# Weighted spreading: ScalarE casts the second part of an older unit ahead of the first part of the new one

## The chip, the core and the metric

One core of a Trainium2 chip runs the whole kernel. The time is the device time of one execution in microseconds; the number shown is the median of three runs.

## What is computed

Four graph layers over 12500 nodes with 48 features and 400000 edges, each as `x = x + layer(relu(layernorm(x)))`. All of them gather rows of a node table by one end of the edges, in places weight them, and add them up at the other end:

```python
xw = jnp.matmul(x, w)                                   # layer 0, edge_src = src
msgs = adj_vals[:, None] * xw[edge_src]
agg = jax.ops.segment_sum(msgs, edge_dst, num_segments=N_NODES)
...
for _ in range(NUM_LAYERS):                             # layer 2, two times
    x = spmm(edge_index, edge_weight, x, n)             # x[src] * edge_weight, summed by dst
    avg = avg + x * scale
...
def prop(h):                                            # layer 3, three times
    return jax.ops.segment_sum(w[:, None] * h[row], col, num_segments=n)
```

Layer 1 has a gate network on the edges beside it. Values are float32.

## The kernel before

Edges lie in blocks of 128 slots x 8 (a block has one window of 128 source nodes). Each gather of a layer is one call of `expand`, called a **spread** here: matmuls with one-hot matrices pick rows of the node table, the rows go to a staging buffer, and indirect stores put them in the order of the destinations into device memory. Each sum is a call of `collect`, which loads them in that order and adds them up with one-hot matmuls. Three spreads are **weighted**: layer 0 (width 80: 48 features and 32 extra columns, `extra`, stored as float32) and the two of layer 2 (width 48). They are followed by three **unweighted** spreads of layer 3, whose staging takes another branch of the same code.

Float32 values are carried by three bfloat16 parts whose sum is the value, since matmuls take bfloat16. A table has the three parts, so a pick is three matmuls added in PSUM. In a weighted spread the picked row is then multiplied by the edge weight, and the product has to be split in three parts again. A spread has 47 turns (`TURNS`) of 6 chunks (`RC`), a chunk is 2 blocks of 128 rows (`CH`) and 2 **units** (`UC`), 564 units in all. What happens to unit u:

- VectorE compares the chunk's loaded places with the partition number: one-hot matrices (`compare`, L1313, once a chunk). SyncE loads the places (L1226, a ring of 3 chunks where there are extra columns, else of 6).
- PE writes one identity matmul of 512 columns into the bank (L1263), then 24 one-hot matmuls (L1272), each 48 or 80 columns. There are `NW` banks: 2 in the first weighted spread, 3 in the others. Before them it waits until the bank's former unit is weighed (and, in the first spread, its extra columns copied).
- VectorE multiplies by the weight into `times`, another PSUM bank of four (`weigh`, L1322).
- ScalarE copies the extra columns (L1369, first spread only), and casts the product to bfloat16: the **first part** (`first_term`, L1372).
- PE subtracts the first part from the product in PSUM (**less-first**, `less_first`, L1244), in the program after the one-hot matmuls of unit u + 2.
- ScalarE casts what is left: the **second part** (`second_term`, L1377).
- VectorE subtracts that and casts: the **third part** (`third_term`, L1332).
- POOL issues an indirect store for each of the chunk's two blocks of 128 rows (L1412), one for each unit, when both units have their third part. Rows of padding are out of bounds and dropped.

The order on each engine is written out by hand in `turn`, with semaphores counting units: VectorE runs at step u the third part of unit u - 5 and then the weighing of unit u - 2; ScalarE handles at step u the first part of unit u and the second part of unit u - 2; PE the matmuls of unit u and less-first of unit u - 2. Each engine takes its instructions in this order.

Of the kernel before, what the change touches and what calls it, by code (L numbers as in the profile page):

```python
# [65 lines left out]
def gnn_kernel(nc, x, src, dst, edge_attr, edge_weight, node_type, node_vec, w0, b0, w1, b1, w2, b2,  # L66
# [56 lines left out]
    with ctx:  # L123
# [1048 lines left out]
        def expand(table, width, weighted, to_dram):  # L1172
# [20 lines left out]
            with ExitStack() as s:  # L1193
# [25 lines left out]
                with nc.Block() as block:  # L1219
# [144 lines left out]
                    def _(act):  # L1364
                        def first_term(i, first, c, n):
                            u = c * UC + n
                            act.wait_ge(x_times, i * UT + (bw + u + 1))
                            if extra:
                                act.copy(stage[:, c, n, ROW // 2:length].rearrange(  # L1369
                                            "p (a k f) -> p a k f", a=2, f=extra),  # L1370
                                         rows_of(u, D, width)).then_inc(x_extra, 1)
                            act.copy(terms(c, n, 0), left(u)).then_inc(x_first, 1)  # L1372

                        def second_term(i, c, n):
                            u = c * UC + n
                            act.wait_ge(x_rest, i * UT + (bw + u + 1))
                            act.copy(terms(c, n, 1), left(u)).then_inc(x_second, 1)  # L1377

                        def turn(i, first):
                            for c in range(RC):  # L1380
                                if not first:
                                    act.wait_ge(x_st[c], i * (16 * CH) + e * (TURNS * 16 * CH))
                                act.copy(row_d[:, c, :], idx_d[:, bass.ds(i * RG + c * CH, CH)]).then_inc(x_row, 1)
                                for n in range(UC):
                                    if weighted:
                                        first_term(i, first, c, n)
                                        u = c * UC + n
                                        if u >= 2:
                                            second_term(i, *before(u, 2))
                                        elif not first:  # L1390
                                            second_term(i - 1, *before(u, 2))
                                    elif n % 2 == 0:
                                        act.copy(*copy_out(act, i, first, c, n)).then_inc(x_out[0], 1)  # L1393
                        turns(act, TURNS, turn)
# [524 lines left out]
```

## Time and profile before

| | |
|---|---|
| median of 3 runs | 19425.97 us (19371.97 to 19426.68) |
| the profiled execution | 19498.8 us |
| its span, first to last instruction | 19497.0 us |
| busy: PE, VectorE, ScalarE, POOL | 12039.6, 12685.6, 5081.6, 7739.5 us |
| mean granted TensorE clock | 0.808 |
| weighted spreads | 7075 to 8342, 11229 to 12343, 12945 to 14064 us |

The profile is of one execution. A time in it is counted from the first instruction; PE is TensorE, DVE VectorE, ACT ScalarE, SP SyncE. A row of a group gives the line, the engine, the operation and its tiles, the number of instructions, their busy time and mean, and the engine's idle time just before them with what ended most of it. The names of the profile for the tiles: `exp_rows` is the picked rows in PSUM, `exp_times` the product, `exp_stage` the staging buffer, `h` the one-hot matrices.

### The profile page before, as it was taken

Reading aid. Unit: us, or ns where it says so; the run is one execution under the profiler, and the core shown is the slowest. Engines: PE = TensorE matmul, PEld = TensorE weight load, DVE = VectorE, ACT = ScalarE, POOL = GpSimd, SP = SyncE. Lnnn points to the kernel's source line nnn. Section 1 sums busy time; section 2 is a strip of 40 time slices with the busy share of each in tenths; the row PEclk is TensorE's granted clock in tenths of the full one; section 3 lists DMA queues with packets and bytes.
Section 4 is the critical chain, followed back from the end, with each engine's and each line's share of the span. In section 5 each row is a group of like instructions: output and inputs, shape, how many; then the busy total and the mean of one; then the engine's idle time right before and its main releaser. Section 6 shows DMA issues by size and latency. Waiting matters only on the chain. (4 is left out here: it accounts for less than half of the span.)

```text
span 19497.0 us, 597789 instructions
## 1 busy us (share of the span) xinstructions
PE 12039.6 (62%) x200859; PEld 9977.6 (51%) x203067; DVE 12685.6 (65%) x26741; ACT 5081.6 (26%) x14023; POOL 7739.5 (40%) x7745
## 2 busy tenths in 40 slices
PE   5666666666660056676776666666675676666667
PEld 4555555555550035564554545554564465455456
DVE  8555555555552246678997866776686676667666
ACT  0222222222222135502442044124303302311320
POOL 0555555555556624402331055125405613622640
PEclk7888888888875579998888988998895596588569
DMA  7444444444445648787998777777697888878877
GB/s 295 157 156 155 156 155 156 156 156 155 156 148 161 138 154 282 245 280 275 338 331 235 248 258 261 237 268 261 213 305 255 286 270 276 298 252 273 299 255 246
DMA packets 2039788, 4485.05 MB, mean 230 GB/s; under 512 B 383651, under 2 KB 820609, under 8 KB 2038903
## 3 DMA queue, kind: packets, MB, share of 16 engines
q1 hardware_dynamic: 1422358, 3108.06, 50.3%
q0 software_dynamic: 437168, 1034.15, 14.1%
q10 hardware_dynamic: 180144, 341.27, 4.8%
q8 instruction: 74, 1.21, 0.0%
q14 instruction: 44, 0.35, 0.0%
HBM read 2732.28 MB, written 2060.98 MB: 246 GB/s over the span
## 5 line engine op out<-in xcount | busy, mean ns | idle before, releaser
L1412 POOL DMA_INDIRECT messages<-exp_stage,exp_block_rows x2820 | 2992.9, 1061 | 5357.6 <-ACT exp_stage L1393 2403.5
L817 POOL DMA_INDIRECT records<-rec,row_i x3125 | 2992.0, 957 | 2868.1 <-DVE rec L683 2105.2
L1513 PE MATMUL sum_sums<-sum_slots,sum_onehot 128*128 128x48 bf16 (+1 forms) x94752 | 2728.4, 183 | 947.3 <-DVE h L1477 700.0
L1513 PEld LDWEIGHTS sum_sums<-sum_slots,sum_onehot 128*128 128x128 bf16 x94752 | 2569.5, 96 | 1227.8 <-issue 1226.3
L1278 PE MATMUL exp_rows<-tab,h 128*128 x13536 | 1843.8, 313 | 1214.3 <-issue 596.4
L1272 PE MATMUL exp_rows<-tab,h 128*128 x40608 | 1733.4, 194 | 1051.7 <-DVE exp_times L1322 430.3
L1278 PEld LDWEIGHTS exp_rows<-tab,h 128*128 128x128 bf16 x13536 | 1385.3, 136 | 1672.3 <-issue 1667.1
L737 PE MATMUL ps_l<-place,turned 98*128 98x98 f32 x6250 | 1131.3, 346 | 1745.2 <-ACT place L622 1741.2
L737 PEld LDWEIGHTS ps_l<-place,turned 98*128 98x128 f32 x6250 | 1019.1, 250 | 1832.7 <-issue 1832.7
L1272 PEld LDWEIGHTS exp_rows<-tab,h 128*128 128x128 bf16 x40608 | 1589.4, 100 | 500.6 <-issue 296.1
L683 DVE TENSOR_TENSOR rec<-ps_g,emeta 128x240 f32<-128x240 f32 x625 | 254.8, 408 | 2188.0 <-remote 1423.6
L1332 DVE TENSOR_TENSOR exp_stage<-exp_times,exp_stage 128x384 bf16<-128x384 f32 x1692 | 942.8, 557 | 1118.7 <-ACT exp_stage L1377 948.5
L1350 DVE CAST exp_stage<-exp_rows 128x576 bf16<-128x576 f32 x1410 | 1041.6, 754 | 909.0 <-PE exp_rows L1278 840.9
L1393 ACT CAST exp_stage<-exp_rows 128x576 bf16<-128x576 f32 x1692 | 1072.1, 639 | 1781.4 <-PE exp_rows L1278 1407.8
L1313 DVE TENSOR_SCALAR h<-exp_places,pcol 128x2048 bf16<-128x2048 bf16 x1692 | 1315.8, 778 | 31.9 <-DMA exp_places<-src_places 31.7
L624 ACT CAST turned<-ps_t 98x640 f32<-98x640 bf16 x625 | 432.5, 692 | 3306.9 <-remote 2852.6
L1765 POOL DMA_INDIRECT messages_back<-l_back,l_rows x564 | 556.3, 986 | 1590.2 <-ACT l_back L1642 842.7
L1372 ACT CAST exp_stage<-exp_times 128x384 bf16<-128x384 f32 x1692 | 812.9, 480 | 1225.6 <-DVE exp_times L1322 1029.2
L1483 DVE TENSOR_TENSOR sum_onehot<-sum_iota,drel 128x2048 bf16<-128x2048 bf16 x846 | 1035.6, 1224 | 61.4 <-issue 47.6
L1483 DVE TENSOR_TENSOR sum_onehot<-sum_iota,slots 128x2048 bf16<-128x2048 bf16 x846 | 1035.8, 1225 | 56.2 <-issue 44.7
L656 DVE SCALAR_TENSOR_TENSOR same<-win_row,emeta,lt_b 128x128 bf16<-128x128 bf16 x3125 | 1064.3, 341 | 1.6 <-DMA win_row<-src_windows_of_edges 1.6
L1477 DVE TENSOR_TENSOR h<-h,sum_sums 128x48 f32 x3384 | 683.0, 202 | 530.3 <-PE sum_sums L1513 275.7
(298 smaller groups left out, 21297.7 us busy)
## 6 DMA issues: line engine op xcount, KB each, us to landing
exp_places<-src_places SPq DMA_DIRECT2D x1692, 512.0 KB
sum_slots<-messages SPq DMA_DIRECT2D x1410, 576.0 KB, 5.2
messages_first<-fill SPq DMA_DIRECT2D x624, 375.5 KB
sum_slots<-messages_back SPq DMA_DIRECT2D x282, 600.0 KB, 5.2
messages_back<-fill ACTq DMA_DIRECT2D x624, 270.8 KB
sum_slots<-messages_first SPq DMA_DIRECT2D x282, 576.0 KB, 5.4
messages<-fill ACTq DMA_DIRECT2D x624, 260.0 KB
l_places<-dst_places SPq DMA_DIRECT2D x282, 512.0 KB
```

What stands on the lines that cost most here:

```text
L656: last = dve.scalar_tensor_tensor(out=same[:, g, j, j * P:(j + 1) * P], in0=win_row[:, g, j * P:(j + 1) * P], scalar=f[:, j, SWIN:SWIN + 1 ...
L737: last = pe.matmul(at(k), turned[0:W, bank[g], k * P:(k + 1) * P], place[0:W, :], start=False, stop=True, skip_group_check=True)
L817: pool.indirect_dma_start(rec_dram, bass.IndirectOffsetOnAxis(ap=row_i[:, g, k:k + 1], axis=0), rec[:, g, k, :], None).then_inc(put[g], 16)
L1272: last = pe.matmul(rows_at(u, a, k), of, flat[:, bass.ds(ws[g] * (3 * width) + j * width, width)], start=j == 0, stop=j == 2)
L1278: last = pe.matmul(got[:, u % NW, k // 2, at:at + 3 * D], of, flat[:, bass.ds(ws[g] * (3 * D), 3 * D)], start=True, stop=True)
L1313: dve.tensor_scalar(onehot[:, c % RS, :, :].rearrange("p n e -> p (n e)"), places[:, c % RP, :], pcol1[:, :], None, ALU.is_equal).then_inc ...
L1332: dve.tensor_tensor(terms(c, n, 2), left(u), terms(c, n, 1), ALU.subtract).then_inc(x_third, 1)
L1350: dve.tensor_copy(*copy_out(dve, i, first, c - 1, n)).then_inc(x_out[1], 1)
L1393: act.copy(*copy_out(act, i, first, c, n)).then_inc(x_out[0], 1)
L1412: pool.indirect_dma_start(to_dram, bass.IndirectOffsetOnAxis(ap=row_d[:, c, g:g + 1], axis=0), stage[:, c, g, :], None, bounds_check=last_ ...
L1483: dve.tensor_tensor(onehot[:, c % RS, :, :].rearrange("p n (e b) -> p n e b", b=2), iota[:, :].rearrange("p (e b) -> p e b", b=2).unsqueeze(1)
L1513: last = pe.matmul(sums[:, c % RS, g, 0:width], onehot[:, c % RS, g * B + k, :], of[:, n * width:(n + 1) * width], start=n == 0, stop=n == ...
```

## The change

Two statements of ScalarE's `turn` change places (the empty line stands in the changed file, and line numbers behind it grow by one).

```diff
--- before.py
+++ after.py
@@ -1383,12 +1383,13 @@
                                 act.copy(row_d[:, c, :], idx_d[:, bass.ds(i * RG + c * CH, CH)]).then_inc(x_row, 1)
                                 for n in range(UC):
                                     if weighted:
-                                        first_term(i, first, c, n)
+
                                         u = c * UC + n
                                         if u >= 2:
                                             second_term(i, *before(u, 2))
                                         elif not first:
                                             second_term(i - 1, *before(u, 2))
+                                        first_term(i, first, c, n)
                                     elif n % 2 == 0:
                                         act.copy(*copy_out(act, i, first, c, n)).then_inc(x_out[0], 1)
                         turns(act, TURNS, turn)
```

At step u ScalarE now first casts the second part of unit u - 2, then copies the extra columns and casts the first part of unit u. What stands in ScalarE's program in the first weighted spread, before (`exp_weighted` counts weighed units, `exp_less_first` less-first matmuls; a row with no wait follows the one above):

```order
L1383 COPY exp_block_rows<-idx_d 128x2
L1369 COPY exp_stage<-exp_rows 128x256 [waits exp_weighted]
L1372 CAST exp_stage<-exp_times 128x8x48
L1377 CAST exp_stage<-exp_times 128x8x48 [waits exp_less_first]
L1369 COPY exp_stage<-exp_rows 128x256 [waits exp_weighted]
L1372 CAST exp_stage<-exp_times 128x8x48
L1377 CAST exp_stage<-exp_times 128x8x48 [waits exp_less_first]
```

and with the change:

```order
L1383 COPY exp_block_rows<-idx_d 128x2
L1377 CAST exp_stage<-exp_times 128x8x48 [waits exp_less_first]
L1369 COPY exp_stage<-exp_rows 128x256 [waits exp_weighted]
L1372 CAST exp_stage<-exp_times 128x8x48
L1377 CAST exp_stage<-exp_times 128x8x48 [waits exp_less_first]
L1369 COPY exp_stage<-exp_rows 128x256 [waits exp_weighted]
L1372 CAST exp_stage<-exp_times 128x8x48
```

The cast L1377 with its wait for less-first stands before the copy L1369 with its wait for the weighing, and the row number copy L1383 stays at the head of each chunk. In the two later weighted spreads, before:

```order
L1383 COPY exp_block_rows<-idx_d 128x2
L1372 CAST exp_stage<-exp_times 128x8x48 [waits exp_weighted]
L1377 CAST exp_stage<-exp_times 128x8x48 [waits exp_less_first]
L1372 CAST exp_stage<-exp_times 128x8x48 [waits exp_weighted]
L1377 CAST exp_stage<-exp_times 128x8x48 [waits exp_less_first]
```

and with the change:

```order
L1383 COPY exp_block_rows<-idx_d 128x2
L1377 CAST exp_stage<-exp_times 128x8x48 [waits exp_less_first]
L1372 CAST exp_stage<-exp_times 128x8x48 [waits exp_weighted]
L1377 CAST exp_stage<-exp_times 128x8x48 [waits exp_less_first]
L1372 CAST exp_stage<-exp_times 128x8x48 [waits exp_weighted]
```

Here too L1377 moves ahead of L1372. VectorE's order in the same loop, which is the same in both kernels (`exp_second` counts second parts, `exp_rows` PE's units, `exp_load` the loads of places):

```order
L1313 TENSOR_SCALAR h<-exp_places,pcol 128x2048 [waits exp_rows,exp_load0]
L1332 TENSOR_TENSOR exp_stage<-exp_times,exp_stage 128x8x48 [waits exp_second]
L1322 TENSOR_TENSOR exp_times<-exp_rows,slots 128x384 [waits exp_third,exp_rows]
L1332 TENSOR_TENSOR exp_stage<-exp_times,exp_stage 128x8x48 [waits exp_second]
L1322 TENSOR_TENSOR exp_times<-exp_rows,slots 128x384 [waits exp_third,exp_rows]
```

The third part L1332 waits for ScalarE's second part, and the weighing L1322 of the next unit stands behind it.

## Rows read from the trace of the kernel before

**Rows 1.** The page, costliest groups: count, busy, mean ns, idle before.

```profile
L1332 DVE TENSOR_TENSOR exp_stage<-exp_times,exp_stage 128x384 bf16<-128x384 f32 x1692 | 942.8, 557 | 1118.7 <-ACT exp_stage L1377 948.5
```

**Rows 2.** The waits of the whole span: us in total, times, longest.

```profile
DVE exp_stage L1332 <- ACT exp_stage L1377: 948.5, 1134, 1.2
```

**Rows 3.** Timeline of the first spread: start us, us, engine, line.

```profile
7600.70 0.97 POOL L1412 DMA_INDIRECT messages_first<-exp_stage,exp_block_rows  x1 [0.30 <-issue]
...
7600.83 0.33 PE L1244 MATMUL exp_times<-exp_stage,less_ident_b 128*128 128x384 bf16 x1
...
7601.90 0.38 PE L1263 MATMUL exp_rows<-tab,ident_b 128*128 128x512 bf16 x1 [0.74 <-ACT exp_stage L1369]
...
7602.55 0.56 DVE L1332 TENSOR_TENSOR exp_stage<-exp_times,exp_stage 128x384 bf16<-128x384 f32 x1 [0.36 <-ACT exp_stage L1377]
7603.03 0.56 DVE L1322 TENSOR_TENSOR exp_times<-exp_rows,slots 128x384 f32<-128x384 f32 x1
...
7603.06 0.33 PE L1244 MATMUL exp_times<-exp_stage,less_ident_b 128*128 128x384 bf16 x1
7603.62 0.37 ACT L1369 COPY exp_stage<-exp_rows 128x256 f32<-128x256 f32 x1 [1.01 <-DVE exp_times L1322]
7603.89 0.48 ACT L1372 CAST exp_stage<-exp_times 128x384 bf16<-128x384 f32 x1
...
7604.10 0.10 PEld L1263 LDWEIGHTS exp_rows<-tab,ident_b 128*128 128x128 bf16 x1 [0.97 <-issue]
...
7604.26 0.50 ACT L1377 CAST exp_stage<-exp_times 128x384 bf16<-128x384 f32 x1
...
7604.78 0.56 DVE L1332 TENSOR_TENSOR exp_stage<-exp_times,exp_stage 128x384 bf16<-128x384 f32 x1 [1.20 <-ACT exp_stage L1377]
```

**Rows 4.** Timeline of the last weighted spread, columns as in rows 3.

```profile
13300.61 0.49 PE L1244 MATMUL exp_times<-exp_stage,less_ident_b 128*128 128x384 bf16 x1
...
13302.14 0.56 DVE L1332 TENSOR_TENSOR exp_stage<-exp_times,exp_stage 128x384 bf16<-128x384 f32 x1 [0.93 <-ACT exp_stage L1377]
...
13302.61 0.56 DVE L1322 TENSOR_TENSOR exp_times<-exp_rows,slots 128x384 f32<-128x384 f32 x1
...
13303.20 0.48 ACT L1372 CAST exp_stage<-exp_times 128x384 bf16<-128x384 f32 x1 [1.10 <-DVE exp_times L1322]
...
13303.25 0.49 PE L1244 MATMUL exp_times<-exp_stage,less_ident_b 128*128 128x384 bf16 x1
...
13303.58 0.48 ACT L1377 CAST exp_stage<-exp_times 128x384 bf16<-128x384 f32 x1
...
13304.09 0.56 DVE L1332 TENSOR_TENSOR exp_stage<-exp_times,exp_stage 128x384 bf16<-128x384 f32 x1 [0.27 <-issue]
...
13304.96 0.49 PE L1244 MATMUL exp_times<-exp_stage,less_ident_b 128*128 128x384 bf16 x1
```

**Rows 5.** Stretches: busy us (instructions) PE, PEld, DVE, ACT, POOL; clock, DMA, GB/s.

```profile
7200.00:8200.00 1000.00, 619.51 (x11373) 516.74 (x11596) 647.26 (x1115) 526.37 (x1563) 433.69 (x447) 1.00 0.79 278
13000.00:13900.00 900.00, 559.77 (x11568) 450.87 (x11796) 623.49 (x1133) 410.05 (x1133) 487.87 (x454) 0.89 0.78 261
14800.00:15600.00 800.00, 508.29 (x3704) 381.51 (x3704) 486.32 (x696) 313.71 (x695) 486.94 (x463) 0.55 0.85 291
9000.00:9500.00 500.00, 366.11 (x4886) 256.17 (x4884) 460.29 (x1033) 244.96 (x658) 184.33 (x188) 0.87 0.98 344
8400.00:8900.00 500.00, 386.32 (x12665) 343.82 (x12790) 417.53 (x787) 0.00 (x0) 0.00 (x0) 0.99 0.90 307
```

**Rows 6.** DMA share in slices of 25 us: 7300 to 8300, 13000 to 14000.

```profile
DMA  8778887787777877888777887887878887843333
...
DMA  7877777777877777777777777777788777787444
```

**Rows 7.** Lines L1412 and L1332: count, ns, first and last start us.

```profile
L1412 POOL DMA_INDIRECT messages_first<-exp_stage,exp_block_rows x564: 966/972/1300, 7083.9 to 8342.4; - x188
...
L1332 DVE TENSOR_TENSOR exp_stage<-exp_times,exp_stage x1692: 547/557/559, 7080.3 to 14063.5; 128x384 bf16<-128x384 f32 x188
```

## Prediction

> **What bounds the kernel now.** I read the page first, then the waits, then short timelines of the stretches that the change touches, then the busy time by stretch. On the page no engine fills the span, so the question is which wait ends last in the three weighted spreads. The costliest idle time in front of a VectorE instruction of these spreads stands before the third part (L1332): 1118.7 us over 1692 units [rows 1], of which the waits put 948.5 us down to ScalarE's cast of the second part (L1377) [rows 2]. The timeline of the first spread shows the ring that sets the pace [rows 3]. The third part starts at 7602.55, the weighing behind it at 7603.03, ScalarE's copy of the 32 extra columns at 7603.62, the first part at 7603.89, the second part at 7604.26, and the next third part at 7604.78: 0.48 + 0.59 + 0.27 + 0.37 + 0.52 = 2.23 us a unit. In the later two spreads the same ring without the extra copy takes 0.47 + 0.59 + 0.38 + 0.51 = 1.95 us [rows 4]. The stretches agree: 1000 us hold 447 units of the first spread (2.237 us each), 900 us hold 454 of a later one (1.982 us) [rows 5], one indirect store being one unit. A spread has 564 units [rows 7].
>
> The reader is to see one thing in rows 3: the second part that starts at 7604.26 had its input long before. PE leads by one unit, so the less-first matmul that this cast waits for is the one at 7600.83 (0.33 us), and ScalarE then stood idle for 1.01 us before 7603.62. The cast was ready, but stood in the program behind the first part of a newer unit, which waits for the weighing.
>
> **What the change takes away.** Nothing is added or removed: 1692 casts L1377 of 0.49 us change places with what stood before them (1692 casts L1372, and 564 copies L1369 in the first spread). No DMA, no semaphore and no buffer changes. The moved cast now runs in ScalarE's idle 1.01 us, beside the weighing. Two links leave the ring: VectorE's third part no longer follows extra copy, first part and second part, and with its input there it starts right behind the weighing. Cost of the cast in its new place: it holds ScalarE for 0.37 us from start to start; if it begins before the weighing ends it delays nothing. What is queued behind it is the extra copy, which frees PE's bank (the first spread has two). What remains is the ring over those two banks: 1.16 us from the identity load (7601.90) to the end of the unit's matmuls, where less-first starts (7603.06), a hand-off to VectorE, 0.59 us from the weighing to the extra copy, and about 0.5 us from that to the next identity load, 2.25 us and the hand-off. No row shows PE handing on to a VectorE that waits for it; the nearest are VectorE to ScalarE, 0.03 us after the end (7603.59 to 7603.62), and a whole matmul of 0.33 us with it, 0.36 us. I take the middle: 2.45 us for two units, 1.22 us each, and at either end under the bounds of the next part, so it costs nothing. If the extra copy is pushed back by the cast's full 0.37 us as well, the ring gives at most (2.61 + 0.37) / 2 = 1.5 us.
>
> **What is late next.** The gain ends where another limit takes over. Busy time per unit in the first spread: VectorE 647.26 / 447 = 1.45 us, PE 1.39, ScalarE 1.18; in a later one VectorE 623.49 / 454 = 1.37, PE 1.23, ScalarE 0.90 [rows 5]. POOL issues a store each 0.97 + 0.30 = 1.27 us [rows 3]. And the DMA: the share is 0.79 at 2.237 us a unit, so a unit costs 1.767 us of all 16 engines; in a later spread 0.78 x 1.982 = 1.546 us [rows 5]. These are larger than any engine's sum, so **the DMA becomes the bound**. How full can it be? The stage that sends messages back holds 0.98, the collect after the first spread 0.90 with nothing waiting on loads there that I could name; these are the nearest rows for the two ends [rows 5]. I take 0.97, near the first, because the loads of places are issued three chunks ahead in the first spread and six in the later ones, and the stores have six chunks of room, so that queues hold work all the time. That gives 1.767 / 0.97 = 1.82 us and 1.546 / 0.97 = 1.595 us a unit.
>
> The Trainium skill, "DMA: Bandwidth & Descriptors", section Specifications, gives about 358 GB/s as what the memory gives one core. The row at 0.98 moved 344 GB/s, a little under it [rows 5]. By that page's figure the estimate would be 278 x 2.237 / 358 = 1.74 us and 261 x 1.982 / 358 = 1.44 us a unit, and the gain some 920 us in place of the 735 below.
>
> At the end of each spread the DMA share falls to 0.3 to 0.4 (stores of padding rows are dropped): the last 6 slices of 25 us of the first spread and the last 3 of a later one [rows 6]. From 8150 to the last store at 8342.4 are 190 us or 86 units, from 13925 to the last third part at 14063.5 are 138 us or 70 units [rows 6, 7]. There the engine sums hold: 1.45 and 1.37 us.
>
> **The sum.** First spread: 478 units x (2.237 - 1.82) = 199, and 86 x (2.237 - 1.45) = 68: 267 us. Each later spread: 494 x (1.982 - 1.595) = 191, and 70 x (1.982 - 1.37) = 43: 234 us, twice 468. Together 735 us. The profiled execution took 19498.8 us, which gives 18764; it lies 73 us above the median of the runs shown, 19425.97, from which I subtract: **18691, rounded 18690 us**. The unweighted spreads and the collects are untouched: 0.
>
> The ends. With the DMA at 1.00 the units cost 1.767 and 1.546 us: gain 225 + 68 + 2 x (215 + 43) = 809. In the unweighted spreads, which move the same bytes, a unit costs 800 / 463 x 0.85 = 1.469 us of DMA against 1.546 [rows 5]; with packets that much (5%) quicker in both: 1.68 and 1.47 us, gain 334 + 2 x 296 = 926, time 18500. With 0.92 as a ceiling: 152 + 68 + 2 x (149 + 43) = 604, time 18820.
>
> **Rivals.**
> 1. *The spread settles at the pace of the unweighted one*, which has no such ring, the same bytes, and yet takes 1.728 us a unit at a share of 0.85 [rows 5]. For it: it is a measured pace with this traffic. Against: its clock is at 0.55, so PE is slower there than here. With a ceiling of 0.85: 2.08 us in the first spread and 1.728 in the later ones, gain 75 + 68 + 2 x (126 + 43) = 481, time 18945.
> 2. *The DMA does not bind*, the transfers fit under VectorE's 1.45 and 1.37 us: gain 564 x 0.787 + 2 x 564 x 0.612 = 1134, time 18290. Against it stands the share of 0.79, which would have to go to 1.22. The Trainium skill, same page and section, gives a fabric ceiling of 435 GB/s; by it a unit would need 1.43 and 1.19 us of DMA and this rival would hold. The highest row here, 344 GB/s at 0.98, speaks against it.
> 3. *The cast's wait only changes place.* ScalarE takes its instructions in order, and the moved cast waits for PE's less-first matmul; if PE loses its lead of one unit, this matmul comes only after the newest unit's matmuls, and the first part and extra copy stand behind it. The third part then gets its input as late as now: 0, time 19426. Against: idle 1.01 us before the extra copy, less-first done 3.1 us before the cast starts [rows 3]. The Trainium skill, "TensorE: Matmul & The Clock Gate", section on the array's architectural detail, says that ScalarE's queue is strictly first in, first out; that is the rule that speaks against putting a waiting cast in front.
> 4. *Slower: the clock.* The granted clock was 1.00 in the first spread, 0.89 in a later one, 0.55 in the unweighted ones [rows 5]. At the lower level (1.2 GHz) PE in a later spread needs 1.71 us between two less-first matmuls (13303.25 to 13304.96) and 4.35 us for two units with the window load between (13300.61 to 13304.96), 2.18 us each [rows 4]. Should the new rhythm hold the clock at the lower level through all three spreads: later ones + 0.2 x 1128 = + 224; the first, whose 24 matmuls have 80 columns for 48, about 2.18 + 24 x 32 / 1200 = 2.8 us at most, + 0.58 x 564 = + 330. Half of the sum of 554, some 275 us, gives 19700. It decides from a mean clock of about 0.6 downwards. Against it: PE's idle share shrinks with the change, it does not grow.
>
> **How the numbers follow.** DMA ceiling between 0.92 and 1.00, quicker packets included (18500 to 18820): 0.66. Rival 1: 0.15. Rival 2: 0.08. Something between 1 and 3: 0.03. Rival 3: 0.05. Rival 4: 0.03. The range, 18480 to 18960, takes in the forecast and rival 1. A measurement of this kernel can tell 0.3% (58 us) from no change. Faster by more: 0.66 + 0.15 + 0.08 + 0.03 = 0.92; same 0.05; slower 0.03.
>
> **What would show it.** In the changed profile the wait of L1332 for L1377 is gone or under 100 us; L1377 starts before L1372 of the newer unit and during the weighing; the DMA share of both spreads is 0.93 or more, at 1.8 and 1.6 us a unit; a new wait appears, VectorE's comparison (L1313) for the load of places, or ScalarE and SP for stores; the clock of the later spreads is above 0.89. I am wrong if the share stays near 0.8 (then an engine ring that I took for slack binds), or if L1332 still waits for ScalarE.

## The result and the profile after

| | before | changed |
|---|---|---|
| median | 19405.66 us (4 runs, 19371.97 to 19426.68) | 19631.73 us (4 runs, 19629.64 to 19639.83) |
| ratio, 95% interval | 1 | 1.0123 (1.0106 to 1.0139) |
| span of the profiled execution | 19497.0 us | 19627.9 us |
| mean granted clock | 0.808 | 0.795 |

The forecast was 18690 us, in a range of 18480 to 18960. The change is slower, by 226 us, where a gain of 735 us was predicted. The wait that I set out to remove is gone, but the spreads got longer. The waits of the whole span with the change (us in total, times, longest) answer to [rows 2]; line numbers behind L1391 have grown by one:

```profile
ACT exp_stage L1377 <- PE exp_times L1244: 1399.4, 549, 5.8
...
DVE exp_times L1322 <- PE exp_rows L1272: 1156.8, 502, 5.5
...
DVE exp_stage L1332 <- ACT exp_stage L1377: 19.3, 36, 1.2
```

The third part's wait for the second part fell from 948.5 us [rows 2] to 19.3. In its place ScalarE waits 1399.4 us for PE's less-first matmul and VectorE's weighing 1156.8 us for PE's one-hot matmuls. In the kernel before the first of these two does not occur and the second is small (waits of the whole span, kernel before):

```profile
DVE exp_times L1322 <- PE exp_rows L1272: 11.7, 16, 1.1
```

On the page of the changed kernel, in the columns of [rows 1]:

```profile
L1272 PE MATMUL exp_rows<-tab,h 128*128 x40608 | 1974.3, 202 | 535.6 <-issue 522.5
```

The stretches, columns as in [rows 5]:

```profile
7200.00:8200.00 1000.00, 726.81 (x10868) 560.60 (x10868) 568.76 (x1044) 498.84 (x1462) 412.99 (x418) 0.85 0.74 260
13100.00:14000.00 900.00, 617.33 (x10969) 443.36 (x10970) 573.50 (x1055) 399.82 (x1055) 417.39 (x421) 0.87 0.72 242
```

The first spread does 418 units in 1000 us (2.39 us each, 2.237 before), a later one 421 in 900 (2.14 us, 1.982 before). The DMA share fell, from 0.79 to 0.74 and from 0.78 to 0.72; I had wanted 0.93 or more. The clock fell in the first spread from 1.00 to 0.85.

What happens inside is seen in the timeline. First a good stretch of the first spread (start us, us, engine, line, in brackets the idle time before it):

```profile
7602.27 0.55 DVE L1332 TENSOR_TENSOR exp_stage<-exp_times,exp_stage 128x384 bf16<-128x384 f32 x1
...
7602.47 0.49 ACT L1377 CAST exp_stage<-exp_times 128x384 bf16<-128x384 f32 x1
...
7602.74 0.56 DVE L1322 TENSOR_TENSOR exp_times<-exp_rows,slots 128x384 f32<-128x384 f32 x1
7603.20 0.55 DVE L1332 TENSOR_TENSOR exp_stage<-exp_times,exp_stage 128x384 bf16<-128x384 f32 x1
```

Here everything is as the prediction has it: second part L1377 beside the weighing, third part L1332 right behind it, two third parts 0.93 us apart. Now the stretch 12 us earlier, in which two units pass through PE:

```profile
7589.38 1.11 PE L1272 MATMUL exp_rows<-tab,h 128*128 x24
...
7590.33 0.33 PE L1244 MATMUL exp_times<-exp_stage,less_ident_b 128*128 128x384 bf16 x1
...
7590.50 0.38 PE L1263 MATMUL exp_rows<-tab,ident_b 128*128 128x512 bf16 x1
7590.71 0.70 PE L1272 MATMUL exp_rows<-tab,h 128*128 x15
...
7591.61 0.23 PE L1272 MATMUL exp_rows<-tab,h 128*128 x2 [0.20 <-issue]
7592.36 0.28 PE L1272 MATMUL exp_rows<-tab,h 128*128 x3 [0.52 <-issue]
...
7593.09 0.30 PE L1272 MATMUL exp_rows<-tab,h 128*128 x4 [0.46 <-issue]
7593.23 0.33 PE L1244 MATMUL exp_times<-exp_stage,less_ident_b 128*128 128x384 bf16 x1
7594.64 0.48 ACT L1377 CAST exp_stage<-exp_times 128x384 bf16<-128x384 f32 x1 [4.22 <-PE exp_times L1244]
7594.83 0.57 DVE L1322 TENSOR_TENSOR exp_times<-exp_rows,slots 128x384 f32<-128x384 f32 x1 [4.07 <-PE exp_rows L1272]
...
7595.95 0.38 PE L1263 MATMUL exp_rows<-tab,ident_b 128*128 128x512 bf16 x1 [2.39 <-ACT exp_stage L1369]
```

The weighing at 7594.83 belongs to the first of the two units, whose 24 matmuls stand in one piece and end in the record at 7590.49; the cast at 7594.64 belongs to the less-first matmul that ends at 7590.66. Both consumers stood for 4 us after work that the record calls done. Meanwhile the second unit's 24 matmuls come in pieces, 15, 2, 3 and 4, with gaps in which PE waits for nothing that the profile names ("issue"); its weighing comes at 7595.77. The trace also holds the semaphore events, that is, the moments at which PE's **signal** "this unit's matmuls are done" is raised. The first unit's signal comes at 7594.58, 4.1 us after the recorded end, and the second's at 7594.85, 0.27 us behind it. The kernel before has the same in its later two spreads: of their signals 369 in 886 come less than 0.5 us after the one ahead, where the recorded last matmuls of two units are never less than 0.98 us apart. So the signals come late and in pairs, which is not the recorded pace of the matmuls; what holds them up, no row shows. The unit pace comes from long and short intervals between weighings: in the first spread a tenth are under 0.94 us, half under 1.66, and a tenth over 5.15, where before nearly all were 2.23.

Grouped by me: a unit's last matmul start to the start of its weighing, over 444 middle units of each spread, and the gaps over 0.15 us between the matmuls of one unit, summed over the whole spread (to some 2%):

| spread | unit us | last matmul to weighing, median / 90% | gaps, us |
|---|---|---|---|
| before, first | 2.242 | 2.23 / 2.23 | 0 |
| before, later two | 1.983, 1.987 | 2.02 / 2.22, 2.00 / 2.18 | 127, 138 |
| changed, first | 2.390 | 1.35 / 3.71 | 155 |
| changed, later two | 2.143, 2.137 | 1.87 / 3.88, 1.71 / 3.93 | 279, 301 |

The third column is a wait only where VectorE stood idle. In the changed first spread that is so for 213 of the 444 units (median 1.40, 90% under 4.37 us), in the later two for 190 and 180 (median 3.46 and 3.58 us).

Before, the ring of casts kept VectorE from asking for PE's result until about 2.2 us after its last matmul started. Lateness up to that left no wait. It did leave late signals: in the kernel before, the signal of each chunk's first unit comes 1.33 us (median) after the recorded end in the first spread and 1.5 us in the later two, that of the second unit 0.01 to 0.03 us after it. With the change a tenth of the signals come more than 3.3 to 3.6 us late.

### The profile page after: what moved, and what is told of

Its sections match the earlier page's. It is cut to its first block and busy times, and to the rows that moved or that the text cites. A ratio compares the mean times of both kernels' runs of the same rounds, so it can differ in the third digit from the quotient of the medians.

```text
span 19627.9 us, 599996 instructions
## 1 busy us (share of the span) xinstructions
PE 12795.6 (65%) x203066; PEld 10186.7 (52%) x203067; DVE 12658.7 (64%) x26741; ACT 5140.9 (26%) x14023; POOL 7663.3 (39%) x7745
## 5 line engine op out<-in xcount | busy, mean ns | idle before, releaser
L1413 POOL DMA_INDIRECT messages<-exp_stage,exp_block_rows x2820 | 2906.4, 1031 | 5563.0 <-ACT exp_stage L1394 2440.3
L1278 PE MATMUL exp_rows<-tab,h 128*128 x13536 | 1802.8, 311 | 1202.1 <-issue 484.2
L1272 PE MATMUL exp_rows<-tab,h 128*128 x40608 | 1974.3, 202 | 535.6 <-issue 522.5
L1272 PEld LDWEIGHTS exp_rows<-tab,h 128*128 128x128 bf16 x40608 | 1764.6, 106 | 990.5 <-issue 808.2
L1278 PEld LDWEIGHTS exp_rows<-tab,h 128*128 128x128 bf16 x13536 | 1384.9, 136 | 1619.7 <-issue 1613.0
L1322 DVE TENSOR_TENSOR exp_times<-exp_rows,slots 128x384 f32<-128x384 f32 x1692 | 951.9, 563 | 1413.1 <-PE exp_rows L1272 1156.8
L1313 DVE TENSOR_SCALAR h<-exp_places,pcol 128x2048 bf16<-128x2048 bf16 x1692 | 1367.5, 808 | 32.2 <-DMA exp_places<-src_places 31.4
L1377 ACT CAST exp_stage<-exp_times 128x384 bf16<-128x384 f32 x1692 | 817.1, 483 | 1631.1 <-PE exp_times L1244 1399.4
L1263 PE MATMUL exp_rows<-tab,ident_b 128*128 128x512 bf16 x1692 | 762.3, 451 | 511.6 <-issue 223.7
```

The source lines that it names most:

```text
L1272: last = pe.matmul(rows_at(u, a, k), of, flat[:, bass.ds(ws[g] * (3 * width) + j * width, width)], start=j == 0, stop=j == 2)
L1278: last = pe.matmul(got[:, u % NW, k // 2, at:at + 3 * D], of, flat[:, bass.ds(ws[g] * (3 * D), 3 * D)], start=True, stop=True)
L1313: dve.tensor_scalar(onehot[:, c % RS, :, :].rearrange("p n e -> p (n e)"), places[:, c % RP, :], pcol1[:, :], None, ALU.is_equal).then_inc ...
L1322: dve.tensor_tensor(left(u), rows_of(u, 0, D), ews[:, bass.ds(i * (2 * RG) + 2 * (c * CH + n), 2), :].unsqueeze(3) .to_broadcast([P, 2, BH ...
L1413: pool.indirect_dma_start(to_dram, bass.IndirectOffsetOnAxis(ap=row_d[:, c, g:g + 1], axis=0), stage[:, c, g, :], None, bounds_check=last_ ...
```

## The experiments

After the result three explanations were open: transfers in the way (of PE's instructions, or of its window loads), something in PE's own stream, and the clock. A kernel is named by its label. Where it says "with the change", the kernel is the changed one with that edit. "The kernel before on that chip" is the one timed beside it.

**The first set (e1 to e4, with the change)** makes the transfers of a weighted spread small, takes the window numbers out, or takes matmuls away.

```diff
# e1_small_loads (and e9), SyncE; fewer places than needed are loaded
+ few = CH * P * B if first or not weighted else P
- sp.dma_start(places[:, c % RP, :], ...)
+ sp.dma_start(places[:, c % RP, 0:few], ...)
# e2_small_stores (and e10), POOL; most rows are out of bounds and dropped
- last_block = pool.to_reg(NBLK - 1)
+ last_block = pool.to_reg(P - 1 if weighted else NBLK - 1)
# e3_fixed_windows (and e12, e18), PE; the same windows for every block
- ws = windows(PE_ENGINE, win_s, i * RG + c * CH, CH)
+ ws = (c, c + 7) if weighted else windows(PE_ENGINE, win_s, ...)
# e4_third_of_matmuls (and e11), PE; one of three parts is picked
- for j in range(3):
+ for j in range(1):
```

> The changed kernel, but from the second turn of each weighted spread on the load of places moves 128 of the 2048 columns (one-hot matrices are built from old places, so the messages are not the reference's). In the changed kernel PE stands still for 155, 279 and 300 us inside its groups of 24 matmuls in the three weighted spreads, against 0, 127 and 138 us before, and a spread takes 2.39, 2.14 and 2.13 us a unit. Theory A, the transfers hold PE up (the loads by what they take of memory and of the ways to it): stalls under 30 us a spread, units at 1.5 us in the first and 1.4 us in the others, total about 18500 us. Theory B, PE's instruction stream cannot be supplied faster than this, whatever the DMA does: stalls stay at 250 us or more, units at 2.1 us or more, total 19500 to 19650 us. Theory C, the window load at the head of each chunk sets the pace: the stalls inside groups may go, but a unit stays at 2.0 us or more.

> The changed kernel, but in the weighted spreads the bound of the indirect stores is 128 blocks rows, so nearly all rows are dropped (the sums of these layers are then not the reference's); POOL issues as before. Theory A in the form that the loads alone do it: stalls stay near 155, 279 and 300 us. Theory A in the form that any transfer does it: stalls fall by half or more and a unit to 1.6 to 1.8 us, total about 18900 us. Theory B: no change, total 19500 to 19650 us.

> The changed kernel, but in the weighted spreads PE takes constant windows of the table instead of loading their numbers (other rows are picked, so values are not the reference's): no register load of about 0.54 us and no address arithmetic on PE. Theory C, the window load sets the pace: a unit falls to about 1.6 us, total about 18800 us. Theory B: the stream is shorter by some 10 of 120 instructions a chunk: a unit falls by 0.1 to 0.2 us, stalls stay. Theory A: a unit falls by the 0.3 us a unit that the load leaves open, to 2.1 and 1.85 us, and the stalls inside the groups stay or grow.

> The changed kernel, but a picked row is one bfloat16 part instead of three in the weighted spreads: 8 one-hot matmuls a unit instead of 24 (values lose accuracy). All transfers are as before. Theory B, the supply of PE's instructions: a unit has 22 instructions instead of 54, the stalls go and the unit falls to what the DMA or VectorE allows, 1.6 to 1.85 us, total about 18750 us. Theory A, the transfers hold PE up wherever it is: stalls per spread stay above 100 us, a unit falls by the PE time left out (0.4 to 0.6 us) at most.

Measured: 16379.86, 16330.06, 16450.09 and 16346.72 us. But the kernel before took 17388.26 us there, not 19400: this chip was in another condition, in which every variant looks alike, and the four totals tell nothing about the slower result. I had not foreseen that, and my reading against the 19400 level would have been wrong. What they do show is PE handing on promptly: in e1's first spread the last matmul to the weighing takes 0.36 us at the median and 0.46 at 99%, gaps sum to 2 us, and the units take 1.64 us (1.35 in the later spreads). e3, with all its transfers in place, runs at 1.67 and 1.37 us.

**The second set (e5 to e7)** repeats both kernels, and puts the new order into the first spread alone.

```diff
# e7_first_spread_only, ScalarE's turn
+ if not extra: first_term(i, first, c, n)
  u = c * UC + n
  ... second_term ...
+ if extra: first_term(i, first, c, n)
```

> The changed kernel once more, beside the kernel before. The last four runs were made where the kernel before takes 17388 us, not 19406; so what they show has to be set against the changed kernel in the same place. Theory A, what takes the transfers' time also holds PE up, and that differs from place to place: where the kernel before takes about 17400 us the change is faster, by my sum for DMA at 0.97 to 1.00 about 650 to 800 us, with stalls inside PE's groups under 30 us a spread; where it takes about 19400 the change is slower again by some 200 us. Theory B, PE's instruction supply is the bound whatever the transfers do: slower by about 1% in either place, stalls of 150 us and more in each spread.

> The kernel before, for a profile in the same place as the changed kernel's. Both theories: units of 2.23 us in the first spread and 1.95 to 1.98 us in the others, since the ring through ScalarE's second part sets them. Theory A: where the whole takes about 17400 us no stalls inside PE's groups in any spread (0, 127 and 138 us before); Theory B: 100 us and more in the later two wherever it runs.

> The new order in the first weighted spread only. Theory A in a place of about 17400 us: a gain of 250 to 350 us, the later spreads as before; in a place of about 19400 us: a loss of 60 to 90 us. Theory B: a loss of 60 to 90 us in either.

The changed kernel took 19651.53 us against 19354.99, ratio 1.0146 (1.0129 to 1.0163). e6, which is the kernel before, took 19352.42. e7 took 19425.65, ratio 1.0045 (1.0029 to 1.0061). The ledger closes with e6 and the changed kernel's first profile: the three weighted spreads take 1256, 1108 and 1108 us from first to last store in e6, and 1344, 1202 and 1199 with the change, together 273 us more, of 277.3 us in the spans. In e7 only the first spread is slow (2.364 us a unit, 1.972 in the later ones as before), 71 us in all. So the new order costs time in the first spread by itself and does not slow the others from there; that each of the later two loses some 90 us is the difference between e6 and the changed kernel.

**The third set (e8 to e11, with the change)** repeats three of the edits on a chip where the kernel before takes 19499.34 us.

> The changed kernel beside the shortened ones of this group. Theory A: slower by 1.0 to 1.5% where the kernel before takes about 19400 us, with 150 to 300 us of stalls inside PE's groups a spread; faster by 3 to 5% where it takes about 17400 us, with under 10 us of stalls. Theory B: slower by about 1% in both.

> The changed kernel with loads of places of 128 columns from the second turn on (old places are used, values are not the reference's), in the same place as e8. Where the kernel before takes about 19400 us, Theory A (transfers and PE disturb each other): stalls fall from 155, 279 and 300 us to under 30 us a spread and a unit to 1.65 and 1.35 us, as in e1. Theory B (PE's supply of instructions is slow there by itself): stalls stay above 150 us and a unit above 2.0 us. Where it takes about 17400 us: as e1.

> The changed kernel with nearly all rows of the weighted spreads' stores dropped, in the same place as e8. Where the kernel before takes about 19400 us, Theory A with any transfer: stalls fall by half or more; Theory A with loads alone: they stay; Theory B: stay, unit above 2.0 us. Where it takes about 17400 us: as e2.

> The changed kernel with 8 one-hot matmuls a unit instead of 24 (one of three parts; values lose accuracy), in the same place as e8. Where the kernel before takes about 19400 us, Theory B: the stalls go, and a unit falls to 1.4 to 1.85 us. Theory A: PE has fewer matmuls but is held up wherever it is, a unit falls by the PE time left out, 0.4 to 0.6 us, to 1.6 to 1.9 us, stalls above 50 us. Where it takes about 17400 us: as e4.

The changed kernel took 19896.51 us (ratio 1.0195, 1.014 to 1.025), with small loads 19971.9, with small stores 19903.69, with a third of the matmuls 19246.39. Stretches of e9, e10 and e11:

```profile
7200.00:8200.00 1000.00, 660.63 (x10306) 548.39 (x10510) 550.29 (x1012) 483.31 (x1417) 399.01 (x405) 0.84 0.40 156
```
```profile
7200.00:8200.00 1000.00, 665.18 (x10439) 551.50 (x10641) 555.65 (x1022) 487.37 (x1431) 404.08 (x409) 0.85 0.34 107
```
```profile
7200.00:8200.00 1000.00, 576.23 (x4838) 368.43 (x4920) 664.83 (x1229) 590.17 (x1720) 489.08 (x491) 0.69 0.83 286
```

With the DMA share down to 0.40 and 0.34, the units still take 2.47 and 2.44 us, as they did with all transfers (2.469 in e8), and the gaps in PE's groups sum to 146 and 130 us against 152. That rules the transfers out as the bound, and loads and stores each by itself as what holds PE up; both small at once was not run. The same hold-up stands in e10's timeline: VectorE stands idle for 4.07 us before a weighing at 7604.67, for matmuls recorded as done at 7600.40 whose signal comes at 7604.44.

With 8 matmuls a unit for 24 (e11) the gaps are gone (0 us), the first spread does 491 units in 1000 us, and the kernel is 3.3% shorter than e8 and 1.3% shorter than the kernel before on that chip, at a clock of only 0.69. So **PE's stream binds the changed spreads**, and a lower clock does not undo the gain; fewer instructions, fewer columns and a shorter loop come together in this edit, so it does not say which of them counts. Nor does it take the hold-up away. A unit takes 2.04 us in the first spread (outside what either theory gave, 1.4 to 1.85 and 1.6 to 1.9) and 1.82 in the later ones, where the same program takes 1.62 and 1.36 at the 17400 level (e4), and VectorE still waits for PE, for 571.1 us in the whole span where e4 has 26.6:

```profile
DVE exp_times L1322 <- PE exp_rows L1272: 571.1, 318, 4.3
```

**The fourth set (e12 to e15, with the change)** was to tell apart what in PE's stream does it: window numbers in registers, POOL's stores, or the identity matmul. In e13 the windows are loaded and then replaced by fixed ones; in e14 POOL's loop is `range(RC if not weighted else 0)` and the waits for these stores go; no message of the weighted spreads is stored then; in e15 the identity matmul at L1263 goes, and the one-hot matmuls start their sums by themselves (`start=j == 0`).

> The changed kernel with constant windows on PE in the weighted spreads (other rows are picked, values are not the reference's): no load of window numbers and no addresses from registers. So far, where the kernel before takes about 19400 us: the changed one takes 2.39 to 2.47, 2.13 to 2.2 us a unit whether loads or stores are cut down or not (e9, e10), and matmul results come up to 4.5 us after the last matmul's recorded start, against 0.36 us in e1. Theory B1, PE gets matmuls with register addresses late there: units fall to 1.9 us or less in the first spread and 1.6 or less in the others, no stalls inside groups. Theory B2, PE gets any instruction late there: units fall by 0.1 to 0.3 us, stalls stay. If it runs where the kernel before takes about 17400 us: 1.67 and 1.37 us as in e3.

> As e12, but PE still loads the window numbers, and then uses constants. Tells the register load from the register addresses. Theory B1 in the form of the addresses: as e12. Theory C, the load with what it makes wait (0.54 to 1.4 us once a chunk): as the changed kernel, 2.1 to 2.4 us a unit.

> The changed kernel without indirect stores in the weighted spreads (their messages are left out): POOL does nothing there. Theory D, POOL's work of issuing holds up the others (it was there in e10, where only the rows were dropped): units fall below 1.7 and 1.5 us. Theories B: no change, 2.1 to 2.4 us.

> The changed kernel without the identity matmul of 512 columns ahead of a weighted unit's matmuls. Theory E, PE is bound by its columns, at a lower real rate than recorded: 512 of 2816 and of 2048 columns are gone, units fall by 0.4 to 0.5 us where the kernel before takes about 19400 us. Theories B: 2 of 54 instructions a unit are gone, a unit falls by 0.1 us at most, stalls stay. The granted clock may fall below 0.85, since PE does less.

Measured: 16437.39, 16377.73, 16220.45 and 16506.69 us. The chip, which had taken 19354.99 us for the kernel before in the second set, now took 17433.89, so the condition is not a property of the chip. At this level the fourth set does not tell its suspects apart either. It shows the DMA share that I had predicted; e12:

```profile
5800.00:6300.00 500.00, 394.83 (x7796) 320.19 (x7793) 396.77 (x750) 353.89 (x1049) 323.50 (x300) 1.00 0.99 378
9600.00:10000.00 400.00, 337.00 (x7578) 254.70 (x7573) 382.73 (x729) 273.03 (x730) 306.77 (x294) 1.00 0.99 378
```

The DMA share is 0.99, at 300 units in 500 us and 294 in 400. But other limits lie close behind: e1, whose small loads bring the share down to 0.60 and 0.53, takes 1.64 and 1.35 us a unit for 1.67 and 1.37. Without stores (e14) it is 1.505 and 1.316 us, near VectorE's 1.45 and 1.37 of my sum, with VectorE busy for 0.92 and 0.97 of the time. e15, which leaves out nothing that the result needs, is 5.3% shorter than the kernel before beside it; it is a single run, at the 19400 level it was not tried, and its units (1.74 and 1.45 us) are longer than e12's, so nothing here shows that leaving the identity matmul out helps.

**The fifth set (e16 to e18)** repeats both kernels and puts fixed windows to the test at the 19400 level.

> The changed kernel, with the kernel before timed beside it. Where the kernel before takes about 17400 us: faster by 5 to 6%, about 16450 us, units of 1.67 and 1.37 us with the DMA at 0.99, no stalls (e12 and e13, which differ from it by constant addresses alone, took 16437 and 16378 us there). Where it takes about 19400 us: slower by 1 to 2%.

> The kernel before, for a profile in the same conditions as e16. Where it takes about 17400 us: weighted units still 2.23 and 1.95 us (the ring sets them, not PE), no stalls inside PE's groups, and the time less than 19400 comes from the first stage and the unweighted spreads. Where it takes about 19400: as e6.

> The changed kernel with constant windows on PE in the weighted spreads (values are not the reference's). Where the kernel before takes about 19400 us, which is where it has not run yet: Theory B1, PE gets matmuls with register addresses late there: 1.9 and 1.6 us a unit or less; Theory B2, PE's stream of matmuls is slow there whatever the addresses: 2.1 us or more, stalls stay. Where it takes about 17400 us: 1.67 and 1.37 us as before.

The changed kernel took 19650.37 us against 19368.47, ratio 1.0139 (1.0112 to 1.0165), e17 19416.57, and e18 19563.64. A stretch of the first spread of e18 (e17's holds 447 units at a clock of 1.00, as before):

```profile
7200.00:8200.00 1000.00, 723.69 (x11437) 552.11 (x11435) 600.28 (x1099) 527.22 (x1539) 434.60 (x440) 0.87 0.76 265
```

Fixed windows take 0.10 and 0.05 us off a unit (2.282 and some 2.09, against 2.384 and 2.14 in e16), and the gaps stay (127, 347, 333 us). They are not the cause (B1, register addresses in the matmuls, and C, the window load, are out). But e12 and e18 are one kernel on two chips, and that comparison says most:

| e12 and e18, one kernel | e12 | e18 |
|---|---|---|
| total | 16437.39 us | 19563.64 us |
| unit, first and later weighted spreads | 1.67, 1.37 us | 2.28, 2.09 us |
| gaps inside PE's groups, three spreads | 2, 0, 1 us | 127, 347, 333 us |
| first stage (3125 stores of records) | 4012 us | 5298 us |
| unweighted spreads | 764, 762, 760 us | 948, 957, 955 us |
| the first four collects | 528, 550, 548, 549 us | 528, 549, 549, 549 us |
| messages sent back | 1497 us | 1501 us |

The collects and the sending back, which are full of transfers, do not differ by 0.5%. The first stage and all spreads differ by 24 to 53%. The clock was lower in e18's spreads (0.87, 0.81, 0.79 for 1.00), but of the intervals over 3.5 us between two weighings in the changed kernel's first spread only about a quarter touch a stretch at the lower of the clock's two levels, 1.2 GHz, where the spread spends 29% of its time; in the later two 53 and 43% touch one, with 31 and 25% of the time there. Most long intervals of the first spread lie wholly at full clock, as does the one in the timeline above, so there the clock is not what makes them; in the later two, where long intervals touch the lower level more often than its share of the time, it may add to them.

**What stays open** is why PE's stream is held up, and its results late, in one condition and not in the other. Two more readings narrow it. The page of the changed kernel has few packets that bring instructions, 74 on one queue and 43 on another:

```profile
q8 instruction: 74, 1.21, 0.0%
```

Those of both queues start at 6998 to 7047 us for the first spread and then none before 8370, so no fetch by DMA falls into the loop. And the long intervals prefer places in the program: a turn has 12 units, and in the last weighted spread of the changed kernel the mean interval before a chunk's first unit is 4.22, 2.25, 3.85, 2.19, 3.72 and 2.22 us over the six chunks, alternating, with 1.04 to 1.45 us for the second units. Over some 37 turns that does not come from chance, but a rhythm of two chunks, once begun, would also keep its places, so it need not be the program's places that cause it. How PE is supplied with instructions is one suspect. Against the plain form of it, that PE cannot get them fast enough, stands the first collect: it runs 13536 matmuls in 528 us at both levels, 26 in each us, where the changed kernel's first spread has 11. e11 shortens the loop body and takes matmuls away in one step, and the two were not tried apart. What delays PE's signals is another suspect. Each run comes with a span and a clock, so all were recorded as they ran, and whether recording PE's many small instructions takes part in it was not tried. POOL's issuing (e14) and the identity matmul (e15) ran only at the 17400 level, so they are untested as causes too. The changed kernel without any edit was never seen at that level; that it gains there is argued from e13, whose windows are loaded as before and which took 16377.73 us against 17433.89, and not shown.

## Why the prediction was wrong

- **What bounds the kernel before**: right. The ring third part, weighing, copy, first part, second part held in e6 and e17 to a hundredth (2.236 and 1.973 us a unit, for 2.237 and 1.982).
- **What the change takes away**: right. The cast runs beside the weighing, the wait of the third part is gone (948.5 to 19.3 us), and the moved cast delays next to nothing: with the change ScalarE takes up a newly weighed unit 0.03 us (median) after the weighing ends.
- **The ring that remains**: here the prediction failed. "No row shows PE handing on to a VectorE that waits for it" was true of the rows, and I then bounded the hand-off from PE to VectorE by 0.03 and 0.36 us and wrote that the ring costs nothing. Measured with the change, the time from the last matmul's start to the weighing is 1.35 us at the median and 3.71 at 90% in the first spread. By my own formula, (1.16 + x + 0.59 + 0.5) / 2 us a unit: with 0.36 it gives 1.3, with 1.35 it gives 1.8, with 3.71 it gives 3.0, and the measured mean is 2.39. The mean of x is 1.60 and gives 1.9, so the hand-off is the larger part but not all; gaps inside the groups (155 us over 564 units, 0.27 each) and the clock of 0.85 lengthen the 1.16 as well, and how much of the rest is theirs was not taken apart. That e1 shows 0.36 us too at the 17400 level is luck: I had built it from a less-first matmul and another hand-off. The cause of the failure is that I priced a resource from places where somebody waits for it, and almost no one waited for PE: in the first spread VectorE asked 2.2 us after the last matmul began. The trace of before did have the price. In the 15 places inside a spread where VectorE stood idle for PE, the last matmul had started 2.7 to 3.6 us earlier, and PE's signals were late in every second unit.
- **PE's sum**, 1.39 and 1.23 us a unit: wrong as a bound, because it adds recorded durations. Neither the gaps between pieces of a group nor the time from a recorded end to the moment the result can be used stands in it. A trace of it was in the profile of before and I did not read it: 127 and 138 us of gaps in the later two spreads, which the lead of one unit hid.
- **The DMA becomes the bound**: wrong at this level (0.74 and 0.72, for 0.97). At the other the share is 0.99 as I had it (e12), but with 0.60 and 0.53 (e1) a unit is only 0.03 and 0.02 us shorter, so VectorE and the ring were as near a bound. There a unit costs less of the DMA than my 1.767 and 1.546 us: 1.67 x 0.99 = 1.65 and 1.37 x 0.99 = 1.36 us, since the packets of the loads take 183 ns in the first spread for 217 before. The prediction's end with quicker packets had 1.68 and 1.47. A small misreading goes with it: the share of the first spread falls in the last five slices of [rows 6], from 8175 us on, and not in six; that is worth 4 us of the 735.
- **Rival 1** (the pace of the unweighted spread, 2.08 us) came nearest in kind: it took that pace as a limit that no sum explains. In the table of e12 and e18 that spread differs between the levels too, 948 us for 764. I gave it 0.15, and excused it by its clock.
- **Rival 2** (the DMA does not bind) and **rival 3** (the wait changes place): the wait did move to L1377 for less-first, as rival 3 has it, but because PE is late, not because ScalarE's order blocks: over all three spreads of the changed kernel a weighed unit stood behind an idle L1377 for some 4 us in all. The price of 0 was too low by 226 us. The Trainium skill's rule that ScalarE's queue is first in, first out ("TensorE: Matmul & The Clock Gate", architectural detail) is in agreement with the order seen, and cost nothing by itself: in e3 and e12, with fixed windows at the 17400 level, the same order gains.
- **Rival 4** (slower by the clock, 0.03): right in sign, but its mechanism needed a mean clock of about 0.6, and the spreads had 0.83 to 0.87. What I set against it, that PE's idle share shrinks, came true (PE's recorded busy share went from 0.62 to 0.73 in the first spread, in part because it ran slower), and the clock fell from 1.00 to 0.85 all the same. So that argument did not hold, and why the clock fell is not shown.
- **The memory's limit.** At the 17400 level the stretches moved 378 GB/s at a share of 0.99. The Trainium skill ("DMA: Bandwidth & Descriptors", Specifications) gives some 358 as the memory's limit for one core, half of what two cores share; this kernel's one core went above it, so the measurement decides against it as a limit here. The fabric ceiling of 435 from the same section was not reached.
- Not foreseen at all: that taking a wait away would make the spread slower than the ring it had. The steady ring of 2.23 us gave PE a lead of one unit that absorbed its hold-ups. With the new order VectorE consumes early when it can, the lead is used up, and each hold-up of 3 to 4 us then stands in full, while the few banks hold too few units for the short intervals to make up for it.

The last sentence is the explanation that I hold. Shown of it are that VectorE now stands idle for PE, the late signals and the dependence on PE's matmuls (e11). That the banks keep the short intervals from making up is argued: the later spreads have three banks for two and lose as much (94 and 91 us for 88). And it leaves one thing open: the hold-ups themselves grew. In the first spread of before no signal in the 444 middle units came more than 2.9 us late, with the change a tenth are over 3.3 us, so the new order does something to PE's stream beyond laying its delays bare.

## What to carry to other kernels

A resource that nobody waits for has no price among the waits of a profile: its busy sum is not its pace. Before you remove a wait that gives an engine slack, look at the scatter of that engine's stream (gaps inside a group put down to "issue", the time from a recorded last matmul to a consumer that is already idle, however few such places there are, and to the semaphore event), and take the slack's removal as a rival with a price. Repeat the kernel before beside every experiment: here two chips, or one chip at two times, differed by 11% where the change makes 1 to 2%, and only the repeats told which experiments could be read against the result.

## What the runs showed of the hardware

- One program takes 17400 or 19400 us, with the difference in the first stage and in all spreads, and none in the collects (528 to 560 us either way). One chip was seen at both levels.
- PE's results reach a VectorE that waits 0.36 to 0.46 us after a last matmul's start at the 17400 level (e1, first spread). At the other level it is 0.4 to 4.4 us in the changed kernel's first spread and mostly over 2.5 in the later ones, with gaps of some 0.5 us between matmuls of one group; a DMA share of 0.34 or 0.40 in place of 0.74 makes no difference to it.
- The recorded end of a matmul is not when its signal comes. At the 17400 level the signal follows 0.01 us after it (e13 and e14, 444 middle units of the first spread); in the kernel before at the 19400 level 1.33 us after it in every second unit, and up to 5.2 us with the change.
- One core moved 388 GB/s at a DMA share of 1.00 (e4, 5800 to 6300 us), with 307 units in these 500 us.
- The granted clock of the changed kernel's first spread goes back and forth between full and half (mostly some 10 us at full, then 3.4 or 6.8 at half), where the kernel before keeps the full one all but throughout. In e11, with a third of the matmuls, it is lower still (0.69 in the stretch shown), and the spread is faster.
